# A cross-attention kernel on one core: in the last quarter two of a unit's eight key blocks are summed by TensorE directly, and the projections' list and some planned places change

## The reference

```
Q = x Wq' + bq ; K = c Wk' + bk ; V = c Wv' + bv        # 16 heads of 32
att = softmax(Q K' / sqrt(32)) ; x1 = layernorm((att V) Wo' + bo + x)
phi = elu(x1) ; fc = elu(c)                              # elu(z) = max(z, min(e^z - 1, 0))
KV = sum over context rows of fc (x) c ; ksum = sum of fc
attn = (phi KV) / (phi . ksum + 1e-6) ; out = layernorm(x1 + attn)
```

## Time and profile before

| | before |
|---|---|
| median of 3 runs | 1574.0 us |
| the profiled execution's own time | 1583.65 us |
| its span, first to last instruction | 1581.9 us |
| PE busy | 1477.9 us, 93% |
| DVE busy | 1317.8 us, 83% |
| POOL busy | 1269.1 us, 80% |
| ACT busy | 932.3 us, 59% |
| mean granted TensorE clock | 0.968 |

### The profile page before, as it was taken

The page is one execution under the profiler, slowest core; times in us unless marked ns, Lnnn a source line. Parts: engine busy times, 40 slices in busy tenths (PEclk is TensorE's granted clock), DMA queues, the critical chain, the costliest instruction groups (busy, mean ns, idle before and its releaser), DMA issues.

```text
span 1581.9 us, 29154 instructions
## 1 busy us (share of the span) xinstructions
PE 1477.9 (93%) x9976; PEld 1015.8 (64%) x9976; DVE 1317.8 (83%) x2448; ACT 932.3 (59%) x1892; POOL 1269.1 (80%) x1069
## 2 busy tenths in 40 slices
PE   8998999999999999999999999999999898998986
PEld 5775776667757667566666767667665555555654
DVE  5768878887788898788999889987978889998874
ACT  3445555665666656556665656655756555665563
POOL 0457777777799988877988989987969899899863
PEclk9999999999999999899999999999999999999998
DMA  7646645246344515333552532445241221301000
GB/s 255 198 132 187 227 154 165 87 122 202 98 125 131 147 47 174 97 124 90 188 145 86 167 90 94 136 143 150 90 124 50 72 62 45 103 27 37 26 16 34
DMA packets 136754, 183.70 MB, mean 116 GB/s; under 512 B 19104, under 2 KB 69408, under 8 KB 136608
## 3 DMA queue, kind: packets, MB, share of 16 engines
q1 hardware_dynamic: 134352, 179.22, 37.4%
q10 hardware_dynamic: 2256, 2.63, 0.5%
HBM read 125.18 MB, written 56.62 MB: 115 GB/s over the span
## 4 chain that ended last, share of the span: by engine, by line
PE 53%; DVE 14%; POOL 13%; issue 10%; DMA 5%; ACT 3%; SPq 1%; POOLq 0%; DVEq 0%; ACTq 0%
PE acc L732 9%; PE score L697 9%; PE scoreT L711 9%; PE misc L790 7%; POOL pair_sum L1327 7%; DVE maxes L1071 5%; PE misc L786 4%; PE misc L827 4%; DVE pair_sum L1111 4%; PE misc L802 4%; PE misc L819 3%; DMA stage<-ctxT_in 1%; POOL pair_sum L1336 1%; PE acc L748 1%; ACT p_ring L894 1%
## 5 line engine op out<-in xcount | busy, mean ns | idle before, releaser
L894 ACT ACTIVATE p_ring<-scoreT 128x512 f32<-128x512 f32 x1024 | 595.8, 593 | 465.6 <-PE scoreT L711 459.5
L1071 DVE TENSOR_REDUCE maxes<-score 128x1 f32<-128x512 f32 x1024 | 672.2, 676 | 123.2 <-PE score L697 120.3
L1327 POOL TENSOR_TENSOR pair_sum<-p_ring 128x512 f32<-128x512 f32 x504 | 664.8, 1327 | 129.6 <-ACT p_ring L894 76.3
L697 PE MATMUL score<-k_stack,q_stack 96*128 96x512 f32 x1024 | 535.1, 523 | 36.4 <-DVE maxes L1071 34.2
L711 PEld LDWEIGHTS scoreT<-q_stack,k_stack 104*128 104x128 f32 x2048 | 388.0, 194 | 177.4 <-ACT p_ring L894 89.8
L711 PE MATMUL scoreT<-q_stack,k_stack 104*128 104x256 f32 x2048 | 430.9, 292 | 29.5 <-ACT p_ring L894 24.2
L697 PEld LDWEIGHTS score<-k_stack,q_stack 96*128 96x128 f32 x1024 | 196.0, 191 | 194.1 <-issue 88.7
L732 PE MATMUL acc<-p_ring,v_sb 128*32 128x256 f32 x4096 | 260.3, 397 | 0.0
L1111 DVE TENSOR_TENSOR pair_sum<-pair_sum 128x512 f32<-128x512 f32 x189 | 234.2, 1239 | 24.9 <-POOL pair_sum L1327 24.7
L1336 POOL TENSOR_TENSOR pair_sum<-pair_sum 128x512 f32<-128x512 f32 x189 | 254.7, 1347 | 0.0
L732 PEld LDWEIGHTS acc<-p_ring,v_sb 128*32 128x32 f32 x4096 | 123.6, 113 | 90.6 <-issue 11.3
(11 more groups left out here) (129 smaller groups left out, 1485.1 us busy)
## 6 DMA issues: line engine op xcount, KB each, us to landing
q_stack<-q_dram SPq DMA_DIRECT2D x189, 128.0 KB, 2.6
k_stack<-k_dram SPq DMA_DIRECT2D x93, 256.0 KB, 5.7
w_parts<-w_dram SPq DMA_DIRECT2D x45, 512.0 KB, 5.6
k_dram<-kept_parts SPq DMA_DIRECT2D x28, 512.0 KB, 3.1
q_dram<-kept_parts SPq DMA_DIRECT2D x27, 512.0 KB, 3.1
ctx_nat<-ctx_in SPq DMA_DIRECT2D x32, 256.0 KB, 3.7
v_sb<-v_dram SPq DMA_DIRECT2D x15, 512.0 KB, 4.3
tiles<-x_in SPq DMA_DIRECT2D x27, 256.0 KB, 3.5
```

The costliest lines, as they stand in the source:

```text
L697: pe.matmul(score[k % 3][:], q_stack[0:SPLIT, unit % NQ, j, t * P:(t + 1) * P], k_stack[0:SPLIT, group_of[unit] % 2 * QUAD + j, h * HALF:( ...
L894: act.activation(p_ring[:, n % NP, h * HALF:(h + 1) * HALF], scoreT[k % 2][:], ACT.Exp, scale=SCALE).then_inc(A["exped"], 1)
L1071: dve.reduce_max(maxes[:, unit % 2, t, j, h:h + 1], score[k % 3][:], AX.X).then_inc(V["maxed"], 1)
L1327: pool.tensor_tensor(pair_sum[:, place_of_pair(pair), cols], p_ring[:, (n - 1) % NP, cols], p_ring[:, n % NP, cols], ALU.add).then_inc(L[" ...
```

## The change

New counts by unit: `SHORT = 3 * UB - 2` is unit 46. Units 46 to 62 have three pairs instead of four; PE multiplies their blocks 6 and 7 with ones in the second visit, as it does all of the last unit's. Their third pair's high half is added by POOL (`add_last`) and not by DVE. The functions that count pairs, adds and waits follow from that.

```diff
-    NQ, NP, NO, NX = 3, 7, 19, 3
+    NQ, NP, NO, NX = 3, 7, 21, 3
+    SHORT = 3 * UB - 2
+    def pairs_of(unit):
+        return SLOTS if unit < SHORT else SLOTS - 1 if unit < SUMMED else 0
...
-        projections += [*(("Q", g, cp) for cp in range(2 if b == 1 else 1) for g in groups), *(("V", b, kb) for kb in blocks),
+        projections += [*(("Q", g, cp) for cp in range(2) for g in groups), *(("V", b, kb) for kb in blocks),
                         *(("K", g, 0) for g in groups), *(("K", g, 1) for g in groups),
-                        *(("V", b, kb + KT // 2) for kb in blocks), *(("Q", g, 1) for g in groups if b > 1)]
+                        *(("V", b, kb + KT // 2) for kb in blocks)]
...
-        unused = sb("unused", [P, D])
...
-            if k // 2 % 2 == 0 and k < UT * SUMMED:
+            p = k % UT // 4
+            if k // 2 % 2 == 0 and p < pairs_of(k // UT):
                 take("POOL", k + LEAD + 4, 13)
-            if k % 4 == 0 and k % UT > 0 and k < UT * SUMMED:
+            if k % 4 == 0 and 0 < p < pairs_of(k // UT):
                 take("POOL", k + LEAD + 6, 13)
-                take("DVE", k + LEAD + 7, 10)
+                take(*(("POOL", k + LEAD + 7, 13) if p == 2 and k >= UT * SHORT else ("DVE", k + LEAD + 7, 10)))
...
-                return FIRST if n < 3 * UB // 2 else 280 + 19 * (n - 3 * UB // 2) // 2
+                return FIRST if n < 3 * UB // 2 else 280 + 10 * (n - 3 * UB // 2)
...
-                return earliest(kind, i) + 56 if earliest(kind, i) > FIRST else FIRST
+                return earliest(kind, i) + 36 if earliest(kind, i) > FIRST else FIRST
...
-            return use, k + 3
+            return use, k + (3 if k < UT * UB + UT else 5)
...
-            phi_of[i] = book("phi", "DVE", max(grow_of[i], end_of.get(("T", i - 1), FIRST), dot_of.get(i - 1, FIRST)) + 1, 10, i)
-            dot_of[i] = book("dot", "DVE", phi_of[i] + 1, 13, i)
+            phi_of[i] = book("phi", "DVE", max(grow_of[i], end_of.get(("T", i - 1), FIRST)) + 1, 10, i)
...
-            take("DVE", end, cost[1])
+            take("DVE", end + (kind == "P"), cost[1])
...
-                    put = send("put_kept", end + 1, turn_of_kept[what], 2, False)
+                    put = send("put_kept", end + 2, turn_of_kept[what], 2, False)
...
             elif kind == "T":
+                dot_of[i] = book("dot", "DVE", end + 2, 13, i)
...
+                if kind == "A" and k < dot_of.get(i, LATE):
+                    return False
...
-                if unit >= SUMMED:
+                if unit >= SHORT:
                     for s in range(VISIT):
                         n = VISIT * v + s
+                        if n % KT < 2 * pairs_of(unit):
+                            continue
                         for j in range(QUAD):
                             mm = pe.matmul(acc[j * DK:(j + 1) * DK, CH:2 * CH], ones[:, 0:DK],
...
+                if unit >= SHORT:
+                    pe.wait_ge(L["run_last"], unit + 1 - SHORT)
...
-                    if n - NP < KT * SUMMED:
-                        act.wait_ge(L["paired"], 2 * ((n - NP) // 2 + 1))
+                    last, kt = divmod(n - NP, KT)
+                    if kt // 2 < pairs_of(last):
+                        act.wait_ge(L["paired"], 2 * (pairs_until(last) + kt // 2 + 1))
...
             def dot(tile):
-                dve.wait_ge(V["phi_made"], tile + 1)
+                dve.wait_ge(T["phi_turned"], tile + 1)
...
-                    out=unused[:], in0=x_nat[slot_of[tile]], in1=phi_total[:], scale=1.0, scalar=0.0,
+                    out=x_nat[slot_of[tile]], in0=x_nat[slot_of[tile]], in1=phi_total[:], scale=1.0, scalar=0.0,
...
-                if kind == "P" and projections[number_of][0] in "KQ":
+                earlier, at = ended.get(k, (None, 0))
+                if earlier == "P" and at > 1 and projections[at][0] in "KQ":
+                    keep_low(at)
+                if kind == "P" and number_of < 2:
                     keep_low(number_of)
...
-                if 0 <= unit < SUMMED and p > 0 and i == 0:
+                if 0 <= unit < SUMMED and 0 < p < (pairs_of(unit) if unit < SHORT else 2) and i == 0:
                     add_high(unit, p)
...
+            def add_last(unit):
+
+                whole, part = (pair_sum[:, place_of_pair(unit, p), HALF:2 * HALF] for p in (0, 2))
+                pool.wait_ge(L["paired"], 2 * pairs_until(unit + 1))
+                pool.wait_ge(V["run_high"], highs_until(unit + 1))
+                pool.tensor_tensor(whole, whole, part, ALU.add).then_inc(L["run_last"], 1)
...
+                if 0 <= unit < SUMMED and p < pairs_of(unit):
+                    if i < 2:
+                        add_pair(unit, p, i)
+                    elif i == 2 and p > 0:
+                        add_low(unit, p)
+                    elif i == 3 and p == 2 and unit >= SHORT:
+                        add_last(unit)
```

More of the change, by code:

```diff
@@ L37, in build @@
     VISITS = KT * UNITS // VISIT
[L38 to L39 removed]
+    SLOTS = KT // 2
     SUMMED = UNITS - 1
+    SHORT = 3 * UB - 2
     UT = 2 * KT
@@ L52, in half_of, with pairs_until, lows_until, highs_until @@
         return i // (QUAD * TPC), i // TPC % QUAD, i % TPC
-    def place_of_pair(pair):
-        unit, p = divmod(pair, RUN_PAIRS)
+    def pairs_of(unit):
+        return SLOTS if unit < SHORT else SLOTS - 1 if unit < SUMMED else 0
+    def pairs_until(unit):
+        return sum(pairs_of(u) for u in range(unit))
+    def lows_until(unit):
+        return pairs_until(unit) - unit
+    def highs_until(unit):
+        return sum(pairs_of(u) - 1 if u < SHORT else 1 for u in range(unit))
+    def place_of_pair(unit, p):
         return unit % 2 if p == 0 else 1 - unit % 2
@@ L740, in visit @@
                                            p_ring[:, n % NP, j * CH:(j + 1) * CH], start=False,
-                                           stop=n % KT == KT - 1, tile_position=(0, j * DK), skip_group_check=True)
+                                           stop=unit >= SUMMED and n % KT == KT - 1, tile_position=(0, j * DK),
+                                           skip_group_check=True)
                 mm.then_inc(T["weighted"], 1)
@@ L1105, in add_high @@
             def add_high(unit, p):
-                whole, part = (pair_sum[:, place_of_pair(RUN_PAIRS * unit + i), HALF:2 * HALF] for i in (0, p))
-                dve.wait_ge(L["paired"], 2 * (RUN_PAIRS * unit + p + 1))
+                whole, part = (pair_sum[:, place_of_pair(unit, i), HALF:2 * HALF] for i in (0, p))
+                dve.wait_ge(L["paired"], 2 * (pairs_until(unit) + p + 1))
                 if p > 1:
-                    dve.wait_ge(V["run_high"], RUNS * unit + p - 1)
+                    dve.wait_ge(V["run_high"], highs_until(unit) + p - 1)
                 dve.tensor_tensor(whole, whole, part, ALU.add).then_inc(V["run_high"], 1)
@@ L1304, in vector_program @@
                     make_phi(when["phi"][k])
-                pair, i = divmod(k - LEAD - 7, 4)
-                unit, p = divmod(pair, RUN_PAIRS)
-                if 0 <= unit < SUMMED and p > 0 and i == 0:
+                slot, i = divmod(k - LEAD - 7, 4)
+                unit, p = divmod(slot, SLOTS)
+                if 0 <= unit < SUMMED and 0 < p < (pairs_of(unit) if unit < SHORT else 2) and i == 0:
                     add_high(unit, p)
@@ L1315, in gpsimd_program, with add_pair @@
             pool = nc.gpsimd
-            def add_pair(pair, h):
-                n, cols = 2 * pair + 1, slice(h * HALF, (h + 1) * HALF)
+            def add_pair(unit, p, h):
+                n, cols = KT * unit + 2 * p + 1, slice(h * HALF, (h + 1) * HALF)
                 pool.wait_ge(A["exped"], 2 * n + h + 1)
-                unit, p = divmod(pair, RUN_PAIRS)
                 if p == 1 and unit > 0:
                     pool.wait_ge(T["divided"], unit)
-                elif p != 1 and pair > 0 and h == 0:
-                    pool.wait_ge(L["run_low"], RUNS * unit + max(p - 1, 0))
-                elif p != 1 and pair > 0:
-                    pool.wait_ge(V["run_high"], RUNS * unit + max(p - 1, 0))
-                pool.tensor_tensor(pair_sum[:, place_of_pair(pair), cols], p_ring[:, (n - 1) % NP, cols],
+                elif p != 1 and h == 0 and unit + p > 0:
+                    pool.wait_ge(L["run_low"], lows_until(unit) + max(p - 1, 0))
+                elif p != 1 and unit + p > 0:
+                    pool.wait_ge(V["run_high"], highs_until(unit) + max(p - 1, 0))
+                    if p == 0 and unit > SHORT:
+                        pool.wait_ge(L["run_last"], unit - SHORT)
+                pool.tensor_tensor(pair_sum[:, place_of_pair(unit, p), cols], p_ring[:, (n - 1) % NP, cols],
@@ L1328, in add_pair @@
                                    p_ring[:, n % NP, cols], ALU.add).then_inc(L["paired"], 1)
             def add_low(unit, p):
-                whole, part = (pair_sum[:, place_of_pair(RUN_PAIRS * unit + i), 0:HALF] for i in (0, p))
```

(15 more changed lines are left out.)

10 lines of the change are left out of this document (4 added, 6 removed).

## The result

The changed kernel takes 1599.2 us in the median of 4 runs (1594.5 to 1601.6), the kernel before, beside it on the same chip, 1574.3 (1573.15 to 1576.62). The ratio is 1.0149, with a 95% interval of 1.0122 to 1.0176. Forecast was 1556 with a range of 1541 to 1577: wrong in sign and outside the range. The profiled execution took 1596.98 us, its span is 1595.4, its mean granted clock 0.967.

The account below looks back on a forecast made before the run. POOL, with DVE behind it, was taken to bound the last quarter and PE the earlier ones. Terms -14 - 4 - 4 + 4 = -18 us took the 1574.0 us median to 1556, range 1541 to 1577.

Parts of the forecast that it names:

- Who sets the pace in the last quarter: Units 46 to 62: POOL sets the pace, DVE behind it; moving work to PE gives -14 us (ends 0 and -30).
- if POOL is followed everywhere: Rival, units 46 to 62: POOL's chain throughout, the quarter gives 30 us, time 1540; clock could rise; chance 0.15.
- PE is the bound: Rival, last quarter: 14.7 us of new matmuls eat what is released, the quarter gives nothing, time 1570; chance 0.18.
- The list: Projections' new order, spacing and deadline: last values land slightly late for units 32 and 48, +4 us (ends 0 and +25).
- the rival on the slower side: Values land late at PE's first visits of units 32 and 48, price 17 to 25 us, time 1577; chance 0.17.
- edits at nothing: Two more `outT` places, `dot` after T and onto `phi`: no gain or loss, +-5 us allowed for the planner's other places.
- `keep_low` and the put: Both one tick later: DVE takes a maximum first, its wait falls below 15 us, -4 us (ends -12 and +6).
- The end at +6: Slower end for the later put: it leaves a tick, 1.45 us, later and the next keep waits for it.
- The allowance: Staged blocks, 5 ticks for 3 from tick 272: ACT's waits on `stage` fall below 6 us, -4 us (ends -9, +3).
- Output places and tail: Two more `outT` places change nothing, with no DVE wait; the 36.4 us tail stays, over 40 would show the forecast wrong.
- The sum: Whole kernel: -14 - 4 - 4 + 4 = -18 us, median 1574.0 to 1556.

Follow-up runs that it names:

- A alone: Kernel before with only the short units (from unit 46: three pairs, `add_last`, two blocks to the ones): 1549.5 us, ratio 0.9809.
- A, C and E: Kernel before with short units, new projection list (spacing, deadline), `dot` after T and in place, 21 output places: 1590.8 us, ratio 1.0084.
- A and C: Kernel before with the short units and the new projection list, spacing and deadline, nothing else: 1579.9 us, ratio 1.0016.
- The pause for `phi`: Changed kernel with POOL waiting, one tick after each `phi`'s own tick, until DVE has made it: 1582.5 us in 10 runs, ratio 1.0022.
- B, C, D and E: Changed kernel without the short units, all its other parts kept: 1593.2 us, ratio 1.0092 of the kernel before.
- without B: Changed kernel with the staged blocks' allowance of before, 3 ticks instead of 5: 1593.0 us, ratio 1.0084 of the kernel before.
- without C: Changed kernel with the projection list, spacing and deadline of before: 1561.8 us, ratio 0.9884 of the kernel before.
- A, B, D and C alone: Kernel before with one part each: short units 1549.5 us, staged blocks' allowance 1572.6, later `put_kept` 1576.6, projection list with spacing and deadline 1589.2.
- E: `dot` after T and in place, 21 output places; added to the kernel before with short units and new list: 1590.8 us against 1579.9.

## Why the prediction was wrong, step by step

**Who sets the pace in the last quarter: right, and the size too small.** The term was -14; alone it is worth 30 us, the end given as "if POOL is followed everywhere". Of the 34 us between the profiled spans of the kernel before and of A alone, 20.6 are in units 46 to 60 and 5.0 behind them. The working took two thirds of POOL's share and let PE's new matmuls eat 11 to 15 us. But PE had the room for them: its busy time there fell, 292.9 to 287.3 us, with 206 instructions more. The clock helped, 0.96 to 0.99 in those 300 us; this the forecast had named in the rival and given nothing. By these two figures PE spent 26 and 6 us at the lower level, which is an estimate of at most 10 of the 20.6 us. The choice of POOL for the last add was not tested by itself. The rival "PE is the bound" falls for this stretch.

**The list: this step failed, in its mechanism and in its size.** It was +4, from values that land late. In the changed kernel they don't. Its load of batch 2's last values and the visit that needs them stand so:

```profile
795.43 0.40 SPq L1526 DMA_DIRECT2D v_sb<-v_dram  x1
...
812.21 1.92 PE L750 MATMUL acc<-p_ring,v_sb 128*32 128x256 f32 x13
```

The load took 12.7 us to land, twice the 6.4 of the earlier trace rows, and was there at 808.1, 4 us ahead of the visit; batch 3's landed 31 us early. So the rival on the slower side named the right part and nearly the right place, but another load. What lands late there is the block of sources in `stage`, 12.9 us after its issue, and what waits for it is ACT. In two of the variants (without the allowance; A, C and E) the values do come late, by 4.2 and 4.6 us, against 17 to 25 in the rival.

The other half of the step that failed is what stands in the middle of the run. The forecast looked at the earlier trace rows, saw PE idle 3.2% there, and didn't draw that any work moved in costs its whole length. With the list alone this is 7.4 us in units 40 to 46, over half of the instructions projections, and some 3.4 us of output projection in 24 to 34. In the changed kernel the projections' matmuls left the late units too, but for units 34 to 40, which are no longer; in 24 to 34 and 40 to 46 it has as many as A alone, and 7 and 6 more of the output projection. The list alone costs 9.5 us. With the short units it is 1.0016 / 0.9809, 33 us: nearly all that they gave.

**Against A alone, whose span is 47.5 us shorter, the changed kernel's loss splits so:** -5.4 up to unit 24, +15.8 in units 24 to 34, -1.0 in 34 to 40, +15.9 in 40 to 46, +9.5 in 46 to 60, +12.7 after. With A and C the two early stretches give +8.6 and +6.3, units 46 to 60 +12.0 at a clock of 0.97, the end +3.3. So of the 24.4 us between the spans of A and C and of A alone the largest part, 12.0, lies in units 46 to 60 themselves; 8 instructions and the clock, 0.97 for 0.99, explain only a part, and the cause stays open. What is left of the changed kernel's losses lies where its stops are: the load of `stage` and the `phi` at 838 in the first, the put at 1087 in the second, the `phi` at 1494 in the last. The pause for `phi` took 1.3% back, 17 us by the medians and 20 by the ratios. The step "edits at nothing" failed there: `dot` was costed by its own length, and what its move does to DVE's instruction before it wasn't looked at.

**The clock.** By the mean clock of each, the changed kernel spent 2 x 0.033 x 1595.4 = 105 us at the lower level and A alone 2 x 0.020 x 1547.9 = 62. At half speed the 43 us between them are worth at most 21.5 us of the 47.5. The forecast had no term for it.

**`keep_low` and the put: misread.** The forecast had DVE take a maximum first and its wait fall below 15 us. In the diff the call stays in the same tick, and the wait rose from 50.7 to 66.1. With the call really moved it is 23.8, and the whole gains 0.4 to 0.6%, but with a long `phi` less. So the -4 is neither shown nor refuted. The end at +6 (a later put) is one event: a put of 9.3 us behind nine loads, which costs PE 8.0 us once. It came in the kernels with B, C, D and E, and not without B or without C.

**The allowance: right alone (-7 for -4), wrong in the whole (+10).** ACT's waits for `stage` fell from 13.2 to 6.4 us; below 6 was asked.

**Output places and tail: right.** No wait of DVE in front of L1160, and the tail from the last unit's second 32 matmuls with ones is 1595.4 - 1556.0 = 39.4 us for 1581.9 - 1543.7 = 38.2.

**The sum was the last step that failed.** A, B, D and C alone give -30, -7, -4 and +9.5, and E, which was not run alone, from its effect on A and C +11: together -20. The whole is +24. Each edit makes the planner place every chain and booking anew, and which instruction of DVE then meets a run of POOL's without a pause, or which put stands behind loads, is decided there. The terms were no more independent than that.

## What to carry to other kernels

Ask of the stretch that work is moved *into* which engine bounds it: here 28 more matmul instructions in a stretch that PE bounds, 16 of them of projections taken from one that POOL bounds, cost 7.4 us there and gave back 0.5. Where a list of loads changes its order, look at every load that then stands behind a crowd of others, and at who waits for it, not only at the one that was moved. When one edit makes a planner re-plan, price the edits one at a time on the chip and keep the best alone; terms added up had the wrong sign. Look in the profile for single instructions many times their median, and for what stops PE for longer than its buffers last, since the clock then charges for it again.

## What the runs showed of the hardware

A VectorE instruction of 128x512 with both inputs in SBUF, started while a GpSimd add of 1.26 us runs, takes 1.73 to 1.01 us by where it falls in the add, and ends 0.55 us after that add's end; with one input in PSUM 0.69 us at every offset. The Trainium skill, SBUF — State Buffer, section "SBUF: two separate sides", says that whichever of a GpSimd instruction that reads SBUF and a VectorE instruction with two SBUF inputs starts first has the shared pair of ports for its whole instruction and the other blocks. The two small kernels agree: VectorE waits for the end of the add, and the next add takes 1.71 us instead of 1.26. In the full kernel the same kind of instruction stood blocked through up to seven GpSimd instructions, 8.43 us, though each of them kept its 1.26 to 1.29 us; a rule that ends with one instruction doesn't give that, and the measurement decides. A pause of POOL, 0.63 us as it came out, ended such holds at 4.78 us. A 512 KB put took 9.3 us to land behind nine loads, for 3.1 in the median, and a block of sources issued behind a like crowd 10.8 to 12.9 us.
